# A gated recurrence beside eight experts on one core: second biases added in the mixing, mixing scales for eight tiles at once, a small decay product on GpSimd

## The chip, the cores and the metric

One core of a Trainium2 chip. Its engines run side by side: TensorE (PE), VectorE (DVE), ScalarE (ACT), GpSimd (POOL) and the queue engine SyncE (SP); each takes its own instructions in order and waits for semaphores. The metric is the device time of one execution in microseconds. All data are float32.

## What is computed

`x` is [8, 512, 256] (4096 rows in 32 tiles of 128). `xn` is `x` normalised over its last dimension. Two branches read it:

```
# recurrence, 16 heads of 16 per sequence, 512 steps
q = silu(xn Wq); k = l2norm(silu(xn Wk)); v = xn Wv
f = sigmoid(xn Wf1 Wf2); a = -k * sigmoid(xn Wgamma) * f
S = S * f[:, None];  S = S + k[:, None] * (a . S + v);  o = q . S
o = o * sigmoid(xn Wog1 Wog2)          # the output gate
s = layernorm(o) * norm_w @ Wo
# experts: softmax, the best 2 of 8, weights cw normalised
out = sum_e cw[:, e] * (gelu(xn W1[e] + b1[e]) @ W2[e] + b2[e])
g = silu(layernorm(out) * gamma + beta)
result = x + s * g
```

## The kernel before, in words

A tile n of the input holds 16 time steps of all 8 sequences. The first stage (to about 225 us) projects tile after tile: TensorE multiplies, ScalarE takes sigmoids, VectorE and GpSimd finish a record of a, f, k, q, v (REC = 80 numbers a head) for each row, and SyncE stores the record (`spill`, L361) and the sigmoid for the output gate (`og_d`, L364) to DRAM. SyncE loads records back as chunks of 16 steps with (sequence, head) on the 128 partitions (`rbh`).

The recurrence runs on VectorE through all of the kernel, in 32 chunks of 8 pairs of steps; g = 0 to 255 counts the pairs. Pairs 0 to 55 are VectorE's alone (`two_steps`, L1166), and the projection's small VectorE work is woven into the first 29. From pair 56 (chunk SHARED = 7) `two_shared_steps` (L1207) runs: VectorE multiplies the state with the first step's factors (L1216) and sums; GpSimd (`decay_and_read`, L304) makes one product of 512 columns, which holds the decayed state and the second step's product, and a product of 512 for the outputs (`read_both`, L324). VectorE sums GpSimd's second half at L1224, after `wait_ge(s_dec, g + 1)`. Several of VectorE's operands lie in PSUM (`home_a`, `home_u`, `home_o`). A chunk's preparation for these pairs is in GpSimd's `prepare_part` (L570) and VectorE's `prepared_rows` (L1143). The sums for the outputs are L1164.

`route` (L1039) picks the experts; GpSimd scatters each row of x twice to its expert's place in DRAM (L502), until about 358 us. Then the experts: 39 tiles of 256 rows, `expert_tile` (L886 on TensorE, L708 on ScalarE). TensorE makes the hidden layer (L891), turns the next tile's rows (L879), makes the second layer for two halves of 128 rows (L903) and adds the second bias by a product whose factors are one row of ones and b2 (L905). ScalarE scales the result by the row's weight into `ysb`, and GpSimd scatters it (`land`, L521) to `y_d`. GpSimd's order is written out when the kernel is built: after the products of pair g it lands a half tile if `(g - 56) * PAIR_STEP + LAND0` has reached LAND0 plus the tile's number times LAND_STEP; these are planned times, with PAIR_STEP 3.7 and LAND_STEP 15.9, and no engine waits for a clock. The rest is landed at pair 223.

Mixing: when all is landed, ScalarE loads `y_d` in groups of 4 tiles (L752). Per pair of tiles j: TensorE adds the two expert rows by identity products (`add_experts`, L914), ScalarE takes sum and square sum (`moments`, L757), GpSimd the scales (`spreads`, L533), ScalarE normalises (`normed`, L771), TensorE turns (`turn_y`), ScalarE takes silu (`silu_g`), TensorE turns back, ScalarE copies to `x_acc` (`turned_back`). All of one j comes before all of the next one, but moments of j + 1 stand between, and after each j the output of two tiles follows. For the outputs, in the last four chunks (from pair 224, counted as s = 0), VectorE in pair 224 + s gates the loaded row of outputs (`gate_o`, L1104), takes its statistics (`out_stats`), and, LAG = 5 tiles behind, multiplies the output projection by the mixed experts (`gated`, L1118, which waits for TensorE's product L959 and the mixing of that tile); ScalarE normalises and copies the turned rows, GpSimd takes the scales (`out_scales`) and adds x (`sum_up`), SyncE loads and stores.

The functions that the change touches, with the line numbers of the profile:

Of the kernel before, what the change touches and what calls it, by code (L numbers as in the profile page):

```python
# [11 lines left out]
P = 128  # L12
# [7 lines left out]
REC = 5 * HD  # L20
A_, F_, K_, Q_, V_ = (HD * n for n in range(5))
# [3 lines left out]
RING = 16  # L25
# [19 lines left out]
YR = 3  # L45
SR = 4
RB = 3
SHARED = 7
LAND0, LAND_STEP = 390.0, 15.9
PAIR_STEP = 3.7  # L50


def build(nc, x, wq, wk, wv, wgamma, wf1, wf2, wog1, wog2, norm_w, wo,
          wg, bg, w1, b1, w2, b2, gamma, beta, out):
    ctx = ExitStack()
    with ctx:
# [6 lines left out]
        def sem(name):  # L63
# [6 lines left out]
        og_d = nc.dram_tensor("og_d", [NT, P, D], F32, kind="Internal").ap()  # L70
# [19 lines left out]
        b2_sb = sb("b2_sb", [1, E, D])  # L90
# [21 lines left out]
        ogs = work[:, o1 + 6 * D:o1 + 10 * D].rearrange("p (u n) -> p u n", u=RS)  # L112
        ksq = work[:, o1 + 10 * D:o1 + 11 * D]
# [37 lines left out]
        prod_a = sb("prod_a", [P, NP, 3, HD, ROW])  # L151
# [12 lines left out]
        home_a = psT[1][:, 0:NP * HD].rearrange("p (n k) -> p n k", n=NP)  # L164
# [3 lines left out]
        oTs = xTs  # L168
        sel = gw[:, 0, :, :].rearrange("p t e -> p (t e)")
        b2_flat = b2_sb[:, :, :].rearrange("a e n -> a (e n)")  # L170
        f_on = work[:, 0:FR * D].rearrange("p (u d) -> p u d", u=FR)
        fog, fx, f_sg = (work[:, (FR + n * SL) * D:(FR + (n + 1) * SL) * D].rearrange("p (u d) -> p u d", u=SL)
                         for n in range(3))
# [23 lines left out]
        s_og = sem("s_og")  # L197
# [11 lines left out]
        s_ogd = [sem(f"s_ogd{n}") for n in range(RS)]  # L209
# [10 lines left out]
        s_b1t = sem("s_b1t")  # L220
        s_b1 = sem("s_b1")
# [30 lines left out]
        s_o = sem("s_o")  # L252
        s_od = [sem(f"s_od{n}") for n in range(OB)]
        s_fl = [sem(f"s_fl{n}") for n in range(SL)]
        s_mul = sem("s_mul")
# [25 lines left out]
        N_W, N_C = 10, 9  # L281
# [18 lines left out]

        def over_v(row):
            return row.unsqueeze(1).broadcast_to([P, HD, HD])


        def decay_and_read(eng, g):
            n, u = g % NP, g // NP % RB
            wide = [P, 2, HD, HD]
            rows = rbh[:, u, 2 * n:2 * n + 2, :].rearrange("p j c -> p (j c)")[:, F_:2 * REC - F_ + 2 * A_]
            rows = rows.rearrange("p (j c) -> p j c", j=2)[:, :, 0:HD]
            eng.tensor_tensor(prod_a[:, n, 1:3, :, 0:HD], state[:, g % SR, :, :].unsqueeze(1).broadcast_to(wide),  # L310
                              rows.unsqueeze(2).broadcast_to(wide), ALU.mult).then_inc(s_dec, 1)
# [20 lines left out]
        def _(sp):  # L332
# [40 lines left out]
            def store_chunk(c):  # L373
                sp.dma_start(o_w[c], obh[:, c % OB, :, :]).then_inc(s_od[c % OB], 16)
# [945 lines left out]
```

## Time and profile before

| | us |
|---|---|
| median of 3 runs | 1239.25 (1235.51 to 1239.74) |
| the profiled execution | 1238.9, its span 1237.2 |
| VectorE busy | 1119.4 (90%), 3502 instructions |
| TensorE busy | 938.7 (76%) |
| GpSimd busy | 918.9 (74%), products of 512 columns at 1.27 each (L310 x200, L327 x175) |
| ScalarE busy | 395.7 (32%) |
| second bias, L905 | 156 instructions |

The span is 40 slices of 31 us in the page; a digit is the busy share in tenths:

```profile
PE   5798898100029999999999999999999934667663
DVE  3799999999999999999999999999999995988882
POOL 3766666367844888888888888888888884877762
PEclk9888988655559999999999999999999976777787
```

TensorE works in slices 12 to 31 (the experts), VectorE from slice 1 on; in the last eight slices, the mixing and the outputs, no engine is full, and TensorE's granted clock is 0.6 to 0.8 of 2.4 GHz.

### The profile page before, as it was taken

The page shows a single profiled execution, that of the slowest core. Times are in us where ns is not written, and L with a number is a line of the kernel's source. Part 1 is how long each engine was busy: PE and PEld are TensorE (multiplying, and loading weights), DVE is VectorE, ACT ScalarE, POOL GpSimd, SP SyncE. Part 2 cuts the span into 40 slices and gives each one's busy share as a digit, 9 for nine tenths or more (in the row PEclk, how much of TensorE's full clock was granted, in tenths as well). Part 3 has the DMA queues.
Part 4 walks back from the last instruction along what each step waited for, and adds up shares of the span by engine and source line. Part 5 has one row for each costly group of instructions (what it writes and reads, how often), then busy time and mean ns, then how long its engine had stood idle before and what let it go on. Part 6 is the DMA issues. An engine that isn't in the chain of part 4 may idle for free.

```text
span 1237.2 us, 17465 instructions
## 1 busy us (share of the span) xinstructions
PE 938.7 (76%) x3773; PEld 683.6 (55%) x3774; DVE 1119.4 (90%) x3502; ACT 395.7 (32%) x1047; POOL 918.9 (74%) x902
## 2 busy tenths in 40 slices
PE   5798898100029999999999999999999934667663
PEld 2343343000018888778888777888878723445441
DVE  3799999999999999999999999999999995988882
ACT  3444444200003333332232223333322203554552
POOL 3766666367844888888888888888888884877762
PEclk9888988655559999999999999999999976777787
DMA  5666656553335666655666556666666427355322
GB/s 165 194 209 177 213 180 188 140 191 107 111 94 150 191 196 195 195 170 183 191 195 193 174 177 195 196 187 181 183 192 191 120 67 210 93 157 149 99 81 69
DMA packets 247251, 202.60 MB, mean 164 GB/s; under 512 B 141425, under 2 KB 225233, under 8 KB 247185
## 3 DMA queue, kind: packets, MB, share of 16 engines
q1 hardware_dynamic: 170146, 82.81, 25.5%
q10 hardware_dynamic: 70224, 100.49, 24.8%
q0 software_dynamic: 6816, 18.69, 4.6%
q14 instruction: 55, 0.45, 0.1%
q8 instruction: 10, 0.16, 0.1%
HBM read 139.42 MB, written 62.54 MB: 163 GB/s over the span
## 4 chain that ended last, share of the span: by engine, by line
POOL 36%; DVE 27%; issue 16%; PE 7%; DMA 6%; SPq 3%; ACT 3%; POOLq 0%; DVEq 0%; ACTq 0%
POOL prod_q L327 13%; POOL prod_a L310 12%; POOL y_d L530 5%; DMA rec_d<-work 4%; DVE obh L1164 3%; PE psA L959 3%; DVE ubuf L1180 3%; DVE prod_a L1175 2%; PE psF L921 2%; SPq L335 2%; DVE prod_q L316 1%; DVE prod_a L1198 1%; DVE state L1204 1%; DVE outer L1190 1%; POOL cross L583 1%
## 5 line engine op out<-in xcount | busy, mean ns | idle before, releaser
L310 POOL TENSOR_TENSOR prod_a<-state,rbh 128x512 f32<-128x512 f32 x200 | 254.7, 1274 | 96.2 <-DVE state L1237 74.0
L903 PE MATMUL psF<-wts,work 128*128 128x256 f32 x1248 | 289.1, 385 | 3.2 <-ACT work L712 2.0
L891 PE MATMUL psA<-xgT,wts 128*128 128x256 f32 x1248 | 282.3, 384 | 0.9 <-ACT xgT L706 0.8
L891 PEld LDWEIGHTS psA<-xgT,wts 128*128 128x128 f32 x1248 | 235.4, 191 | 45.1 <-issue 13.8
L903 PEld LDWEIGHTS psF<-wts,work 128*128 128x128 f32 x1248 | 230.8, 190 | 50.0 <-issue 16.5
L327 POOL TENSOR_TENSOR prod_q<-state,rbh 128x512 f32<-128x512 f32 x175 | 223.2, 1276 | 0.0
L1164 DVE TENSOR_REDUCE obh<-prod_q 128x16 f32<-128x272 f32 x512 | 217.6, 426 | 0.0
L712 ACT ACTIVATE work<-psA,b_sb 128x256 f32<-128x256 f32 x312 | 130.8, 470 | 162.3 <-PE psA L891 159.5
L1224 DVE TENSOR_REDUCE ubuf<-prod_a 128x16 f32<-128x272 f32 x200 | 86.0, 430 | 37.5 <-POOL prod_a L310 37.1
L723 ACT ACTIVATE work<-psF,work 128x256 f32<-128x256 f32 x78 | 36.9, 473 | 256.9 <-PE psF L905 256.9
L879 PE MATMUL psT<-ident,work 128*128 128x128 f32 x156 | 24.2, 279 | 119.2 <-DMA work<-xs_d 119.1
L484 POOL TENSOR_TENSOR rinv<-ssm,neghalf 128x16 f32<-128x16 f32 x32 | 100.3, 3134 | 2.7
L502 POOL DMA_INDIRECT xs_d<-x_acc,idx x64 | 79.2, 1237 | 19.5 <-issue 18.9
L1237 DVE TENSOR_TENSOR state<-psB,outer 128x256 f32<-128x256 f32 x200 | 84.2, 421 | 5.8
L1216 DVE TENSOR_TENSOR prod_a<-state,psT 128x256 f32<-128x256 f32 x200 | 83.8, 419 | 5.8
L879 PEld LDWEIGHTS psT<-ident,work 128*128 128x128 f32 x156 | 19.2, 143 | 125.6 <-issue 117.9
L530 POOL DMA_INDIRECT y_d<-work,ids x78 | 78.9, 1011 | 12.3 <-issue 10.0
L1219 DVE TENSOR_REDUCE psB<-prod_a 128x16 f32<-128x272 f32 x200 | 86.5, 432 | 0.0
L1222 DVE TENSOR_TENSOR psB<-rbh,psB 128x256 f32<-128x256 f32 x200 | 83.6, 418 | 0.0
L1230 DVE TENSOR_TENSOR psB<-prod_a,psB 128x256 f32<-128x256 f32 x200 | 83.4, 417 | 0.0
L1232 DVE TENSOR_TENSOR outer<-rbh,psB 128x256 f32<-128x256 f32 x200 | 82.4, 412 | 0.0
L845 PE MATMUL psA<-w_kq,xTs 128*128 128x512 f32 x128 | 78.4, 743 | 0.0
(171 smaller groups left out, 1543.3 us busy)
## 6 DMA issues: line engine op xcount, KB each, us to landing
wts<-in_L_ffn_W_dram ACTq DMA_DIRECT2D x78, 1024.0 KB
rec_d<-work SPq DMA_DIRECT2D x32, 640.0 KB
rbh<-rec_d SPq DMA_DIRECT2D x32, 640.0 KB
xs_d<-zero SPq DMA_DIRECT2D x26, 387.0 KB, 9.0
work<-xs_d ACTq DMA_DIRECT2D x39, 258.0 KB
wts<-y_d ACTq DMA_DIRECT2D x16, 512.0 KB, 5.5
x_acc<-in_L_attn_x_dram SPq DMA_DIRECT2D x32, 128.0 KB
og_d<-work SPq DMA_DIRECT2D x32, 128.0 KB, 7.9
```

The source lines that it names most:

```text
L310: eng.tensor_tensor(prod_a[:, n, 1:3, :, 0:HD], state[:, g % SR, :, :].unsqueeze(1).broadcast_to(wide), rows.unsqueeze(2).broadcast_to(wid ...
L327: eng.tensor_tensor(prod_q[:, g % SR, :, :, 0:HD], state[:, g % SR, :, :].unsqueeze(1).broadcast_to(wide), rbh[:, u, 2 * n - 1:2 * n + 1, ...
L484: pool.tensor_tensor(rinv[:, u, :], ssm[:, u, :], neghalf[:, 0:H], ALU.pow).then_inc(s_ng, 1)
L530: pool.indirect_dma_start(y_d, bass.IndirectOffsetOnAxis(ids[:, v, q:q + 1], 0), ysb[v][:, q, :], None).then_inc(s_yd[v], 16)
L712: act.activation(hT[:, m, :], psA[m // 2 % 2][:, m % 2 * MT:(m % 2 + 1) * MT], ACT.Gelu, bias=b1_sb[:, bass.ds(e * FC + m, 1)]).then_inc(s ...
L891: mm = pe.matmul(psA[m // 2 % 2][:, m % 2 * MT:(m % 2 + 1) * MT], w1_sb[v][:, c, m * P:(m + 1) * P], xgT[:, c, :], start=(c == 0), stop=(c ...
L903: pe.matmul(psF[q][:, 0:D], hT[:, m, q * P:(q + 1) * P], w2_sb[v][:, m, :], start=(m == 0), stop=False)
L1164: dve.tensor_reduce(obh[:, c % OB, row % RING, :], prod_q[:, g % SR, side, :, :], AX.X, ALU.add).then_inc(s_o, 1)
L1216: dve.tensor_tensor(prod_a[:, n, 0, :, 0:HD], old, over_v(home_a[:, n, :]), ALU.mult).then_inc(s_chain, 1)
L1219: dve.tensor_reduce(u1, prod_a[:, n, 0, :, :], AX.X, ALU.add).then_inc(s_chain, 1)
L1224: dve.tensor_reduce(raw, prod_a[:, n, 2, :, :], AX.X, ALU.add).then_inc(s_chain, 1)
L1237: dve.tensor_tensor(new, home_o, outer[:, 1, :, :], ALU.add).then_inc(s_chain, 1)
```

## The change

Its parts:

1. b2 is no longer added in `expert_tile`. It lies 4 times per tile group in `b2_sb` [128, 4, 256], zero elsewhere, loaded by 16 small DMAs that SyncE issues after those of the weights and ahead of the first `spill`. `route` also makes the full weights cw of each row; ScalarE and TensorE turn them into `cwT`, and `add_experts` starts each tile's sum with a product of all 128 rows of `cwT` and `b2_sb`.
2. Mixing goes by groups of GQ = 8 tiles. `moments` copies the sum to `x_acc`, so that PSUM is free after the squares; `spreads(q)` makes the scales of eight tiles in one go, at planned times (SPREADS); `normed` reads `x_acc`. The order on ScalarE is: moments of 16 tiles; then for each q: normalise 8 tiles, moments of the 8 tiles two groups on, silu and turning back. The outputs of the first 8 tiles stand beside the silu of the last group (q = 3), the others behind it.
3. In shared pairs VectorE makes both steps' products itself (512 columns), GpSimd only the decayed state (`decay`, 256 columns, into `decayed`). `two_steps` and `two_shared_steps` become one function.
4. The output gate travels in the record (REC = 96), with one sigmoid of 512 columns in place of two of 256. It is applied to a chunk's outputs at once (`gate_outputs`, 256 columns), by VectorE in the chunks up to 7 and the last one, by GpSimd in the others, at the fourth pair of the next chunk; storing a chunk and loading another into its place wait for that. `og_d`, its stores and loads and `gate_o` are gone.
5. PAIR_STEP becomes 3.86, LAND_STEP 15.0; `out_scales` comes one pair later on GpSimd.

```diff
-REC = 5 * HD
-A_, F_, K_, Q_, V_ = (HD * n for n in range(5))
+REC = 6 * HD
+A_, F_, O_, K_, Q_, V_ = (HD * n for n in range(6))
+GQ = 8
+SPREADS = (612.0, 624.0, 640.0, 662.0)
-LAND0, LAND_STEP = 390.0, 15.9
-PAIR_STEP = 3.7
+LAND0, LAND_STEP = 390.0, 15.0
+PAIR_STEP = 3.86
...
+        def gate_outputs(eng, c):
+            eng.tensor_tensor(obh[:, c % OB, :, :], obh[:, c % OB, :, :], rbh[:, c % RB, :, O_:O_ + HD], ALU.mult)\
+                .then_inc(s_og, 1)
-        def decay_and_read(eng, g):
+        def decay(eng, g):
             n, u = g % NP, g // NP % RB
+            eng.tensor_tensor(decayed[:, :, :], state[:, g % SR, :, :], over_v(rbh[:, u, 2 * n, F_:F_ + HD]),
+                              ALU.mult).then_inc(s_dec, 1)
...
-            sp.dma_start(b2_sb[:, :, :], b2.rearrange("(a e) n -> a e n", a=1)).then_inc(s_c, 16)
+            sp.wait_ge(s_pool0, 5)
+            for n in range(P // E):
+                sp.dma_start(b2_sb[n * E:(n + 1) * E, n % 4, :], b2).then_inc(s_c, 16)
...
             def spill(n):
                 u4 = n % RS
-                sp.wait_ge(s_og, n + 1)
-                sp.dma_start(og_d[n], ogs[:, u4, :]).then_inc(s_ogd[u4], 16)
...
-            def spreads(j):
-                lo, hi = 2 * j, 2 * j + 2
+            def spreads(q):
+                lo, hi = q * GQ, (q + 1) * GQ
...
+                if g % NP == GATED and g // NP > SHARED:
+                    pool.wait_ge(s_o, g // NP * RING)
+                    gate_outputs(pool, g // NP - 1)
                 s = g - WOVEN * NP
+                if spread < NT // GQ and ((g - SHARED * NP) * PAIR_STEP >= SPREADS[spread] or s >= 2):
+                    spreads(spread)
+                    spread += 1
...
+            for j in range(2 * half):
+                moments(j)
+            for q in range(NT // GQ):
+                act.wait_ge(s_yr, q + 1)
+                for j in range(q * half, (q + 1) * half):
+                    normed(j)
+                for j in range((q + 2) * half, min((q + 3) * half, NT // 2)):
+                    moments(j)
+                for j in range(q * half, (q + 1) * half):
+                    silu_g(j)
+                    if q < NT // GQ - 1:
+                        if j > q * half:
+                            turned_back(j - 1)
+                    else:
+                        n = 2 * (j % half)
                         out_normed(n)
+                        out_normed(n + 1)
                         out_turned(n)
+                        turned_back(j)
+                        out_turned(n + 1)
...
-                    pe.matmul(psF[q][:, 0:D], ones[0:1, :], b2_flat[:, bass.ds(e * D, D)], start=False, stop=True)\
-                        .then_inc(s_y, 1)
...
                 for n in range(2 * j, 2 * j + 2):
+                    total = sums[j % 2][:, n % 2 * D:(n % 2 + 1) * D]
+                    pe.matmul(total, cwT[:, n // 4, :], b2_sb[:, n % 4, :], start=True, stop=False)
                     for c in range(2):
+                        mm = pe.matmul(total, ident[:, :], yab[:, g % YR, c, n % GM, :], start=False, stop=(c == 1))
...
+                dve.tensor_tensor(prod_a[:, n, :, :, 0:HD], old.unsqueeze(1).broadcast_to([P, 2, HD, HD]),
+                                  coef.unsqueeze(2).broadcast_to([P, 2, HD, HD]), ALU.mult).then_inc(s_chain, 1)
...
+                if homed:
+                    for j, side in enumerate((u1, raw)):
+                        dve.tensor_reduce(side, prod_a[:, n, j, :, :], AX.X, ALU.add).then_inc(s_chain, 1)
...
                 dve.wait_ge(s_dec, g + 1)
+                dve.tensor_tensor(out1, decayed[:, :, :], out1, ALU.add).then_inc(s_chain, 1)
```

## Rows read from the trace of the kernel before

**Rows 1.** Busy us by stretch: PE, PEld, DVE, ACT, POOL, then PE's granted clock, DMA share, GB/s.

```profile
1010.00:1040.00 30.00, 8.96 (x28) 7.12 (x29) 22.66 (x73) 8.57 (x26) 19.60 (x23) 0.61 0.58 158
1100.00:1150.00 50.00, 34.98 (x117) 25.80 (x117) 43.95 (x147) 25.43 (x74) 40.80 (x53) 0.71 0.50 147
```

**Rows 2.** VectorE's timeline, shared pairs: start us, us, engine, line, operation.

```profile
385.06 0.42 DVE L1216 TENSOR_TENSOR prod_a<-state,psT 128x256 f32<-128x256 f32 x1
...
505.61 0.42 DVE L1216 TENSOR_TENSOR prod_a<-state,psT 128x256 f32<-128x256 f32 x1
...
508.72 0.42 DVE L1237 TENSOR_TENSOR state<-psB,outer 128x256 f32<-128x256 f32 x1
509.17 0.42 DVE L1216 TENSOR_TENSOR prod_a<-state,psT 128x256 f32<-128x256 f32 x1
...
1009.10 0.42 DVE L1216 TENSOR_TENSOR prod_a<-state,psT 128x256 f32<-128x256 f32 x1
```

**Rows 3.** TensorE's timeline in one expert tile, around the second bias.

```profile
507.44 0.69 PE L905 MATMUL psF<-b_sb,ones 1*128 x2
508.06 3.72 PE L903 MATMUL psF<-wts,work 128*128 128x256 f32 x16
```

**Rows 4.** Groups by line: busy us, mean ns, idle us before them and its releasers.

```profile
L1224 DVE TENSOR_REDUCE ubuf<-prod_a 128x16 f32<-128x272 f32 x200 | 86.0, 430 | 37.5 <-POOL prod_a L310 37.1
...
L1216 DVE TENSOR_TENSOR prod_a<-state,psT 128x256 f32<-128x256 f32 x200 | 83.8, 419 | 5.8
...
L1175 DVE TENSOR_TENSOR prod_a<-state,rbh 128x512 f32<-128x512 f32 x56 | 37.9, 677 | 0.1
...
L1106 DVE TENSOR_TENSOR work<-work 128x256 f32<-128x256 f32 x32 | 19.7, 617 | 17.2 <-DMA work<-og_d 17.1
...
L321 POOL TENSOR_TENSOR prod_q<-state,rbh 128x256 f32<-128x256 f32 x25 | 18.1, 724 | 0.0
...
L470 POOL TENSOR_TENSOR rstd<-var,neghalf 128x8 f32<-128x8 f32 x3 | 4.9, 1642 | 0.0
```

**Rows 5.** SyncE's and VectorE's timelines before the first pair.

```profile
28.62 0.45 SPq L354 DMA_DIRECT2D b_sb<-in_L_ffn_b_dram  x1
...
31.45 0.63 SPq L368 DMA_DIRECT2D rec_d<-work  x1
37.97 0.36 SPq L371 DMA_DIRECT2D rbh<-rec_d  x1
...
48.22 0.23 DVE L1130 TENSOR_TENSOR cross<-rbh 128x128 f32<-128x128 f32 x1
```

**Rows 6.** The last landing on GpSimd and the first sums on TensorE.

```profile
1012.60 1.01 POOL L530 DMA_INDIRECT y_d<-work,ids  x1 [0.17 <-issue]
...
1024.71 5.79 PE L921 MATMUL psF<-wts,ident 128*128 128x256 f32 x16 [23.94 <-DMA wts<-y_d]
```

**Rows 7.** ScalarE's and TensorE's timelines, two tiles of mixing and two of output.

```profile
1110.30 1.02 ACT L784 ACTIVATE gT<-psT,gb 128x256 f32<-128x256 f32 x2
...
1113.39 2.07 PE L959 MATMUL psA<-wo_sb,xTs 128*128 128x256 f32 x4 [0.47 <-ACT xTs L801]
...
1116.68 1.03 ACT L776 ACTIVATE wts<-psF,ysh,yrs 128x256 f32<-128x256 f32 x2
1119.88 0.38 ACT L763 ACTIVATE junk<-psF 128x256 f32<-128x256 f32 x1 [2.18 <-PE psF L921]
...
1121.91 1.02 ACT L784 ACTIVATE gT<-psT,gb 128x256 f32<-128x256 f32 x2
```

**Rows 8.** VectorE's timeline in the woven pairs 230, 239 and 240, and its last.

```profile
1062.59 0.41 DVE L1216 TENSOR_TENSOR prod_a<-state,psT 128x256 f32<-128x256 f32 x1
...
1108.17 0.41 DVE L1216 TENSOR_TENSOR prod_a<-state,psT 128x256 f32<-128x256 f32 x1
1112.47 0.41 DVE L1216 TENSOR_TENSOR prod_a<-state,psT 128x256 f32<-128x256 f32 x1
...
1209.74 0.41 DVE L1123 TENSOR_TENSOR work<-psA,x_acc 128x256 f32<-128x256 f32 x1
```

More of the change, by code:

```diff
@@ L398, in _ @@
                 sp.wait_ge(s_yd[u], 16 * MH * ((NM + 1 - u) // 2))
-            for u in range(RS):
-                sp.wait_ge(s_ogd[u], 16 * (NT // RS))
             def fetch(n):
@@ L684, in _ @@
             act.wait_ge(s_b1, 1)
+            act.wait_ge(s_cw, 1)
+            act.activation(cw4.rearrange("p n (r k) -> p n r k", r=4),
+                           gw[:, 1, :, :].rearrange("p (n t) e -> p n (t e)", t=4).unsqueeze(2).broadcast_to([P, NT // 4, 4, 4 * E]),
+                           ACT.Copy).then_inc(s_cw4, 1)
+            act.wait_ge(s_cwT, 1)
+            for n in range(2):
+                act.activation(cwT[:, 4 * n:4 * n + 4, :].rearrange("p n t -> p (n t)"), psA[n][:, :], ACT.Copy, scale=0.25)\
+                    .then_inc(s_cws, 1)
             act.wait_ge(s_slot, 2)
@@ L688, in _ @@
                 act.wait_ge(s_recd[u], 16 * (NT // RS))
-            for u in range(RS):
-                act.wait_ge(s_ogd[u], 16 * (NT // RS))
             def expert_of(t):
@@ L872, in _ @@
             pe.matmul(psT[1][:, 0:NT * E], ones[:, :], sel, start=True, stop=True).then_inc(s_cnt, 1)
+            pe.wait_ge(s_cw4, 1)
+            for n in range(NT // 4):
+                mm = pe.transpose(psA[n // 4][:, n % 4 * P:(n % 4 + 1) * P], cw4[:, n, :], ident[:, :])
+            mm.then_inc(s_cwT, 1)
             pe.wait_ge(s_slot, 2)
+            pe.wait_ge(s_cws, 2)
             def turn_rows(t, v, nth):
@@ L960, in out_rows @@
                 mm.then_inc(s_s, 1)
[L962 to L971 removed]
+            half = GQ // 2
+            for j in range(2 * half):
+                add_experts(j)
+            for q in range(NT // GQ):
+                for j in range((q + 2) * half, min((q + 3) * half, NT // 2)):
+                    add_experts(j)
+                for j in range(q * half, (q + 1) * half):
+                    turn_y(j)
+                    turn_back(j)
+                    if q == NT // GQ - 1:
+                        for n in range(2 * (j % half), 2 * (j % half) + 2):
+                            out_rows(n)
+            for n in range(GQ, NT):
                 out_rows(n)
@@ L1184, in two_steps @@
                     sum_row(g - 2, 0)
-                dve.wait_ge(s_chain, done + 2)
-                dve.scalar_tensor_tensor(out=u2, in0=u1, scalar=pair[:, 1, n:n + 1], in1=u2, op0=ALU.mult, op1=ALU.add)\
+                if shared(g):
+                    sum_row(g - 2, 1)
+                dve.wait_ge(s_chain, done + 3)
+                dve.scalar_tensor_tensor(out=u2, in0=u1, scalar=pair[:, 1, n:n + 1], in1=raw, op0=ALU.mult, op1=ALU.add)\
                     .then_inc(s_chain, 1)
-                dve.tensor_tensor(outer[:, 0, :, :], over_v(rbh[:, u, 2 * n, K_:K_ + HD]), over_k(u1), ALU.mult).then_inc(s_chain, 1)
@@ L1234, in two_shared_steps @@
                 if out_tile is not None and out_tile < NT - 1:
                     out_stats(out_tile)
-                dve.wait_ge(s_chain, done + 8)
-                dve.tensor_tensor(new, home_o, outer[:, 1, :, :], ALU.add).then_inc(s_chain, 1)
+                dve.wait_ge(s_chain, done + 7)
+                dve.tensor_tensor(new, out1, outer[:, 1, :, :], ALU.add).then_inc(s_chain, 1)
+                if not shared(g) and g > 1:
+                    sum_row(g - 2, 1)
                 if out_tile is not None and out_tile >= LAG:
```

233 lines of the change are left out of this document (93 added, 140 removed).

## The prediction

> **What bounds the kernel now.** I read the engine shares of the page first: VectorE is busy 90% of the span, TensorE 76%, GpSimd 74%. Then the stages. In the page's 40 slices TensorE and VectorE both stand at nine tenths while the experts run (365 to 1001 us), with VectorE and GpSimd sharing the recurrence. After that neither is full: at 1010 to 1040 us VectorE works 22.7 of 30 us, TensorE 9, and TensorE's granted clock is 0.61; at 1100 to 1150 it is 0.71 [rows 1]. There a pair of time steps takes VectorE 5 to 7 us instead of 3.56. So I followed three clocks: how fast VectorE goes through its 256 pairs of steps, when the last expert rows land, and how long the mixing takes (sum of two expert rows, LayerNorm, silu, turned back), since `gated` makes VectorE wait for the mixing inside the recurrence.
>
> I number pairs g = 0 to 255. Pair 56 (first one shared with GpSimd) starts at 385.06, pair 221 at 1009.10: 3.782 us a pair [rows 2]. A pair without a wait takes 3.56 (505.61 to 509.17), the chunk's preparation adds 1.0 per 8, and the rest, 0.1, is VectorE waiting for GpSimd's product, 37.1 us over the run [rows 2, 4].
>
> **The second bias.** Two fp32 instructions per half tile go, 0.62 us from the first to what follows (507.44 to 508.06), so 1.24 us in each of 39 tiles, 48 us of TensorE [rows 3]. A tile goes by some 16.2 us now; at 15.0 TensorE's last one ends 47 us earlier than 1001, plus what its start is later, by 960. But what lands is paced by GpSimd, which is told 15.0 us a tile from 390: the last two rows go at pairs 204 and 205. In exchange each mixed tile gets one more product with 128 rows, half of what the two identity products are: 2 instructions of 0.22 (the experts' pitch [rows 3]) to 0.45, hidden until the mixing starts.
>
> **VectorE per shared pair.** The first product becomes 512 wide: 677 ns in the stretch where VectorE works alone, against 419 for the one of 256: +0.26 [rows 4]. The other instructions keep their number and sizes. Before, an instruction stood right behind the one it needs twice, at 0.45 from start to start (508.72 to 509.17) instead of 0.33 [rows 2]; now the small product stands between the sum and the new state, so one of these gaps goes. 3.56 + 0.26 - 0.12 = 3.70 to 3.72; with a preparation of 1.0 per chunk (its copy from 128 to 256 columns is 0.1 more, the rest of the chunk's edge as before) 3.845 a pair. GpSimd's decay product shrinks from 512 to 256 columns (0.72 [rows 4]), a gating of the same size is added once a chunk, and VectorE needs the product only 2.8 us into the pair, where it was 1.7: I cost its waits at 0, and at the 0.1 of now if I am wrong. So a pair goes from 3.782 to 3.845: the lighter GpSimd pays for nearly all of the dearer VectorE.
>
> The SBUF page is to be weighed here. The new product reads the state in SBUF and its factors in PSUM beside GpSimd, as the one of 256 did, which took 419 ns in the mean of 200, hardly above the 0.41 of its best [rows 4, 8]: no slowing, so +0.26 stands. (Held by one GpSimd product each time, it would be 0.7 a pair, 140 us; the nearest row says no.) Only the removed gating of a loaded row (`gate_o`, both inputs in SBUF) shows it: 617 ns in the mean [rows 4]. The Trainium skill ("SBUF — State Buffer", section "SBUF: two separate sides") says a VectorE operation with two SBUF inputs and a GpSimd operation exclude each other for a whole instruction; the trace agrees. By that rule the change takes one such case out of each woven pair and adds none.
>
> **Before pair 56.** The sync queue must issue 16 loads for the second bias where one was, each some 0.45 us [rows 5], ahead of the first record's store. That store went at 31.45, its load at 37.97, and VectorE used it at 48.22 without a wait [rows 5]. I put the store at 37.8 and the load, after a record larger by a fifth, at 45. What the load takes isn't shown: with 3 us VectorE isn't late, with 10 it is late by 7. I take 4. Then 6 gatings of a chunk by 0.35 before pair 56 (2.1) and one at pair 59, and the added products of `route`, of which 0.4 are left since VectorE waits there for TensorE anyhow. The two sigmoids in one and the output gates without their own store save ACT and the sync queue work, which VectorE hides: 0, and 2 us at most where records are late around 60 us. Pair 56 starts at 385.06 + 4 + 2.1 + 0.4 = 391.6.
>
> **The mixing.** Landing at pair 205: 391.9 + 149 x 3.845 = 965, and 2 us of products. Before, 12.1 us lay between the last landing's issue (1012.60) and TensorE's first sum (1024.71) [rows 6]; now the first sum is at 979. Pairs of tiles then pass their moments while TensorE does 12 instructions (2.8 us, the first 5.4): all of the first eight are through by 1008, which hides them beside VectorE. But the scales of the first eight tiles are taken by GpSimd at pair 215: 391.9 + 159 x 3.845 = 1003.3, plus its products (1.95) and 2.4 for the scales (the power over 8 columns is 1.64 [rows 4], two small ones around it): 1007.7. From there ScalarE and TensorE alternate in one chain, in an order in which **the first output tile comes after three quarters of the mixing**: `gated(0)`, which VectorE does in pair 229, needs
>
> - normalising 16 pairs of tiles at 0.93 (1.03 for two with their tail overlapped [rows 7]): 14.9
> - moments of the last 8 pairs at 2.1 (1119.88 to 1121.91): 17, and TensorE's cold start in each group of four, 3 each: 23 [rows 6, 7]
> - one load of ScalarE's function table, which I take with 1.3
> - 12 turns of silu: silu 0.93, the previous pair's copy back 0.55, TensorE turns back and turns the next one (1.1 to 1.9 by the clock), handing over 0.3: 2.9 to 3.6, I take 3.2: 38.4; the durations are those of the chain in [rows 7]
> - silu of pair 12, and the first output row: 1110.30 to 1115.46 in the trace: 5.2 [rows 7]
>
> together 82.8, so `gated(0)` at 1090.5. VectorE by its own pace is at pair 224 at 1038 and would want it at 1064: it stands for some 26 us. In the kernel before, pair 230 starts at 1062.59 [rows 8]; now at 1090.9, 28 later.
>
> **The woven pairs after it.** A pair with neither wait nor statistics takes 4.30 now (1108.17 to 1112.47) [rows 8]. The wide product adds 0.26, `gate_o` takes 0.33 away: 4.24; statistics' scales 0.71 per 4 pairs and preparation 1.0 per 8: 4.55. ScalarE and TensorE need 8.4 us for two tiles without moments and normalising (1110.30 to 1121.91 less 3.2 for those), against 9.1 of VectorE, so VectorE sets the pace, where before the chain of 11.6 us per two tiles did. 26 x 4.55 = 118.3: the last pair ends at 1209.2, against 1210.07 before (from pair 230, 147.5) [rows 8]. So the gain of 29 in this stretch pays back the stand of 28. Behind it: gating the last chunk and its wait +0.8, the gate load and `gate_o` of the last tile -0.45. Span 1237.2 - 0.9 + 0.35 = 1236.7. The profiled execution was 1238.9 for its span of 1237.2, 0.35 below the median 1239.25, and I leave that out: **1238 us, no change** that can be measured (about 0.5%, 6 us, is what can be told).
>
> **Rivals.**
> - *The chain of mixing is shorter.* With TensorE at 2.4 GHz in it the turns are 2.7 (-6), the moments 18 (-5), and if the first load isn't late, -4: 1223 to 1228. For it: the 16 first sums take 5.79 [rows 6], so 0.36 each, already between the two clocks after a gap of 24 us. Against: the granted clock was 0.61 and 0.71 in this stage [rows 1], with gaps as now. Chance 0.27.
> - *VectorE never stands at `gated(0)`.* Then pair 230 starts at 1064, and 118.3, 27.5 for what follows the last pair (1237.2 - 1210.07 + 0.35) and 1.7 outside the span give 1212. It needs the 83 us chain done in 56; ScalarE's own work in it is some 60. Chance 0.05.
> - *Slower: the chain is longer*, TensorE at 1.2 GHz through it: turns 3.6 (+5), sums of 5.4 us a pair in the moments (+7), scales of the third or fourth eight tiles late (GpSimd, in order, holds VectorE at pair 226), and the recurrence's start late by 7 (+3). It decides from a chain of 89 us: 1246, and all of it 1253. For it: TensorE runs only short bursts between ScalarE's steps. Chance 0.28.
> - *The 48 us of TensorE reach the end.* That would be 1191. It can't be while the landing waits for pairs of the recurrence; under 0.01.
>
> **Numbers.** Forecast case 0.40, its own range 1233 to 1245. Range of all 1225 to 1252: below lie the case without a stand and a fifth of the first rival, above some of the slower one. Faster than 1233: 0.32; within 0.5%: 0.40; above 1245: 0.28.
>
> **What would show it.** An expert tile of 14.7 to 15.0 us; first product of 0.60 and 3.85 us a pair between pairs 60 and 200, with almost no wait of VectorE for GpSimd; pair 56 at 389 to 395; TensorE idle for some 20 us before 979; ScalarE waiting for the scales until 1008; one wait of VectorE of 20 to 32 us in `gated` at pair 229, for TensorE's output product; 4.5 to 4.7 us a pair behind it. I am wrong if that wait is under 12 us, or if woven pairs stay above 5 us.

## The result, and the profile after

The changed kernel takes 1257.79 us in the median (1256.94 to 1259.01) against 1239.49 for the kernel before beside it: 1.0153 times, 95% interval 1.0136 to 1.0170. I had forecast 1238, and 1225 to 1252 as the range: it is slower by 18 us and lies 6 us above that range. Its profiled execution took 1259.01 with a span of 1257.3, 20.1 longer than before.

Three words are used below. The *stand* is the one long idle time of VectorE at `gated(0)`, in pair 229. *Woven* pairs are those from 224 on, which carry the work on the outputs. A *chunk's edge* is the last pair of a chunk with the preparation of the next.

The page of the changed kernel, busy shares and VectorE's line by slices:

```profile
PE 902.5 (72%) x3689; PEld 684.2 (54%) x3689; DVE 1163.9 (93%) x3482; ACT 403.0 (32%) x1018; POOL 819.5 (65%) x891
...
DVE  3779999999999999999999999999999998299993
```

TensorE has 36 us less to do, GpSimd 99 less, VectorE 44.5 more. In the slices at 1037 to 1069 and 1069 to 1100 us VectorE falls to 8 and 2 tenths: the second is the stand. Behind it VectorE is full again, where it was at 8 and 9 before.

Groups of the changed kernel by line (busy us, mean ns | idle before), to set beside [rows 4]:

```profile
L1206 DVE TENSOR_TENSOR prod_a<-state,psT 128x512 f32<-128x512 f32 x200 | 137.3, 687 | 6.0
...
L1237 DVE TENSOR_TENSOR psB<-decayed,psB 128x256 f32<-128x256 f32 x200 | 84.8, 424 | 2.9 <-POOL decayed L315 2.9
L1175 DVE COPY prod_a<-rbh 128x256 f32<-128x256 f32 x24 | 19.6, 815 | 0.0
L1008 DVE TENSOR_TENSOR lt<-stats 128x4 f32<-128x4 f32 (+3 forms) x14 | 8.6, 617 | 0.0
```

The first product costs 687 against 419, as planned, and VectorE's wait for GpSimd went from 37.1 us to 2.9. The last two groups were no terms of my sum.

VectorE's timeline: pairs 56, 57, 215, 216, 229, what it stood for there, and pairs 230 and 231 (compare [rows 2, 8]):

```profile
396.95 0.69 DVE L1206 TENSOR_TENSOR prod_a<-state,psT 128x512 f32<-128x512 f32 x1
400.65 0.69 DVE L1206 TENSOR_TENSOR prod_a<-state,psT 128x512 f32<-128x512 f32 x1
...
1012.31 0.69 DVE L1206 TENSOR_TENSOR prod_a<-state,psT 128x512 f32<-128x512 f32 x1
...
1074.06 0.69 DVE L1206 TENSOR_TENSOR prod_a<-state,psT 128x512 f32<-128x512 f32 x1
...
1102.00 0.42 DVE L1148 TENSOR_TENSOR work<-psA,x_acc 128x256 f32<-128x256 f32 x1 [23.95 <-PE psA L981]
1102.34 0.68 DVE L1206 TENSOR_TENSOR prod_a<-state,psT 128x512 f32<-128x512 f32 x1
1106.58 0.68 DVE L1206 TENSOR_TENSOR prod_a<-state,psT 128x512 f32<-128x512 f32 x1
```

So pair 56 is at 396.95 (I said 391.6), a plain shared pair is 3.70 as predicted, 159 pairs take 3.870 each (3.845), the stand at `gated(0)` is there and 24 us long (20 to 32), but it ends at 1102.0 and not at 1090.5. A plain woven pair is 4.24, as predicted (1102.34 to 1106.58). Yet the stretch from 1102.34 to the end of the last pair, at 1231.27, is 128.9 and not 118.3.

One thing here belongs to this one execution. Eighteen of the 19 chunk's edges between pairs 56 and 215 take 4.99 to 5.00 us and one, at 674 us, takes 6.67, because a copy in it lasts 2.49 and not 0.82:

```profile
674.41 2.49 DVE L1175 COPY prod_a<-rbh 128x256 f32<-128x256 f32 x1
```

Of the experiments below, those that leave these pairs as they are take 3.857 or 3.858 us a pair and not 3.870. So 1.9 us of every "earlier than the changed kernel" that is read behind pair 215 come from the profile that it is compared with.

The hand-over to the mixing, on GpSimd and ScalarE:

```profile
1016.42 0.22 POOL L543 TENSOR_TENSOR ysh<-ynm,yrs 128x8 f32<-128x8 f32 x1
```

```profile
1009.65 0.20 ACT L780 ACTIVATION_READ_ACCUMULATOR junk<-psF,ynm 128x1 f32 x1
1016.68 3.55 ACT L787 ACTIVATE wts<-x_acc,ysh,yrs 128x256 f32<-128x256 f32 x7 [6.84 <-POOL ysh L543]
```

ScalarE had done the moments of sixteen tiles and then stood 6.84 us for scales that GpSimd makes behind pair 215. From there the chain takes 85.3 us to 1102.0; I had 82.8 from 1007.7.

Set against my sum of 1236.7: scales 9.0 late (5.4 from the start, 3.6 from the pairs, about half of it that one edge), chain +2.5, woven stretch +10.6, tail -1.5 (26.0 us after 1231.27, I had 27.5) make 1257.3. The experiments take these terms, and the stand itself, one by one.

### The profile page after: what moved, and what is told of

The parts are those of the page before. It is cut to its first block, busy times and chain, and to the rows that moved or that the text cites. A ratio compares the mean times of both kernels' runs of the same rounds, so it can differ in the third digit from the quotient of the medians.

```text
span 1257.3 us, 17142 instructions
## 1 busy us (share of the span) xinstructions
PE 902.5 (72%) x3689; PEld 684.2 (54%) x3689; DVE 1163.9 (93%) x3482; ACT 403.0 (32%) x1018; POOL 819.5 (65%) x891
## 4 chain that ended last, share of the span: by engine, by line
DVE 66%; issue 18%; DMA 4%; PE 4%; POOL 3%; ACT 3%; SPq 1%; DVEq 0%; POOLq 0%; ACTq 0%
DVE obh L1191 10%; DVE outer L1229 7%; DVE psB L1215 6%; DVE state L1246 6%; DVE psB L1237 5%; DVE ubuf L1215 5%; DVE prod_a L1206 4%; DMA rec_d<-work 3%; DVE prod_q L1240 3%; DVE ubuf L1217 3%; DVE psB L1225 2%; DVE prod_a L1175 1%; DVE prod_q L321 1%; DVE outer L1237 1%; DVE work L1038 1%
## 5 line engine op out<-in xcount | busy, mean ns | idle before, releaser
L315 POOL TENSOR_TENSOR decayed<-state,rbh 128x256 f32<-128x256 f32 x200 | 145.4, 727 | 227.9 <-DVE state L1246 204.4
L927 PE MATMUL psF<-wts,work 128*128 128x256 f32 x1248 | 277.5, 381 | 0.0
L916 PEld LDWEIGHTS psA<-xgT,wts 128*128 128x128 f32 x1248 | 237.7, 192 | 37.1 <-ACT work L722 4.5
L927 PEld LDWEIGHTS psF<-wts,work 128*128 128x128 f32 x1248 | 235.8, 191 | 30.3
L1206 DVE TENSOR_TENSOR prod_a<-state,psT 128x512 f32<-128x512 f32 x200 | 137.3, 687 | 6.0
L1237 DVE TENSOR_TENSOR psB<-decayed,psB 128x256 f32<-128x256 f32 x200 | 84.8, 424 | 2.9 <-POOL decayed L315 2.9
L1215 DVE TENSOR_REDUCE ubuf<-prod_a 128x16 f32<-128x272 f32 x200 | 85.3, 427 | 0.0
L865 PE MATMUL psA<-w_kq,xTs 128*128 128x512 f32 x128 | 82.4, 778 | 0.0
```

The source lines that it names most:

```text
L315: eng.tensor_tensor(decayed[:, :, :], state[:, g % SR, :, :], over_v(rbh[:, u, 2 * n, F_:F_ + HD]), ALU.mult).then_inc(s_dec, 1)
L916: mm = pe.matmul(psA[m // 2 % 2][:, m % 2 * MT:(m % 2 + 1) * MT], w1_sb[v][:, c, m * P:(m + 1) * P], xgT[:, c, :], start=(c == 0), stop=(c ...
L927: mm = pe.matmul(psF[q][:, 0:D], hT[:, m, q * P:(q + 1) * P], w2_sb[v][:, m, :], start=(m == 0), stop=(m == FC - 1))
L1206: dve.tensor_tensor(prod_a[:, n, :, :, 0:HD], old.unsqueeze(1).broadcast_to([P, 2, HD, HD]), coef.unsqueeze(2).broadcast_to([P, 2, HD, HD] ...
L1215: dve.tensor_reduce(side, prod_a[:, n, j, :, :], AX.X, ALU.add).then_inc(s_chain, 1)
L1237: dve.tensor_tensor(out1, decayed[:, :, :], out1, ALU.add).then_inc(s_chain, 1)
```

## The experiments

Each is the changed kernel with one edit, if nothing else is said. The ratios are to the kernel before, which stood beside them at 1239.86 us (biases, statistics, gating, copies), 1240.51 (`out_scales`), 1242.28 (the doubled decay product, one run of each) and 1240.96 (the others). A gain in us is the difference from the changed kernel's 1257.79, which had 1239.49 beside it. The kernel before thus moved by up to 1.5 us between the series of several runs, and reckoned against it each gain comes out larger, by 0.4 to 1.5 us.

### The loads of the second bias behind the last record

```diff
-            for n in range(P // E):
-                sp.dma_start(b2_sb[n * E:(n + 1) * E, n % 4, :], b2).then_inc(s_c, 16)
...
+            for n in range(P // E):
+                sp.dma_start(b2_sb[n * E:(n + 1) * E, n % 4, :], b2).then_inc(s_b2, 16)
```

The loop leaves its place ahead of the first record's store and stands behind the last record.

> The changed kernel with the 16 loads of the second bias issued by SyncE after the last record instead of ahead of the first. Theory: these loads make the first records late, and the 10 us that the changed kernel is behind at pair 4 (84.55 against 74.59 us) go nearly whole; since the wait of VectorE in pair 229 hangs on the scales taken at pair 215, the end comes earlier by the same: 1248 to 1250 us against 1258. Rival: the larger records (768 KB against 640) make the stores land later, so that half of the 10 us or more stays: 1252 to 1256.

SyncE of the changed kernel, what [rows 5] showed of before, and VectorE's waits:

```profile
28.89 5.91 SPq L361 DMA_DIRECT2D b_sb<-in_L_ffn_b_dram  x16
...
36.75 0.63 SPq L372 DMA_DIRECT2D rec_d<-work  x1
44.28 0.38 SPq L375 DMA_DIRECT2D rbh<-rec_d  x1
```

```profile
DVE work L1038 <- DMA rec_d<-work: 9.7, 3, 6.5
```

The same two views of this experiment:

```profile
31.13 0.63 SPq L371 DMA_DIRECT2D rec_d<-work  x1
38.64 0.38 SPq L374 DMA_DIRECT2D rbh<-rec_d  x1
```

```profile
DVE work L1041 <- DMA rec_d<-work: 4.4, 2, 4.2
```

1250.42 us (1249.15 to 1251.68), ratio 1.0083 [1.0061, 1.0105]: 7.4 less than the changed kernel. Pair 56 comes at 390.91, 6.0 earlier, and every stage behind it moves with it. Of the 10.0 us at pair 4 (84.55 against 74.59), 5.7 go (78.89) and 4.3 stay, so the loads were a little more than half of it and not nearly the whole, as I had expected; the rival's larger records are the likely rest. So sixteen small DMAs on a queue that feeds VectorE cost their full 6 us. My sum had let VectorE absorb some of that, because the first load had not been waited for. But the wait falls on later records: VectorE waits for a record's store to leave the slot in `work` (L1038), in all 9.7 us. With the loads gone 4.4 us of it stay; before it was 0.5. What has changed there besides is the record, a fifth larger, so I put these down to it; no run took it back by itself.

### The output scales told before the new state

```diff
+                for q, (lo, hi) in enumerate(NORMS):
+                    if out_tile is not None and out_tile == hi - 1 and hi < NT:
+                        out_spread(q)
                 dve.wait_ge(s_chain, done + 7)
                 dve.tensor_tensor(new, out1, outer[:, 1, :, :], ALU.add).then_inc(s_chain, 1)
...
-                for q, (lo, hi) in enumerate(NORMS):
-                    if out_tile is not None and out_tile == hi - 1 and hi < NT:
-                        out_spread(q)
```

> The changed kernel with VectorE's out_spread (seven small instructions, in every fourth woven pair) issued ahead of the new state instead of behind it, where GpSimd stands idle. Theory: the two additions of two SBUF inputs (0.59 and 0.69 to 1.23 us now, 0.15 before the change) are held by GpSimd's products, which start when the state is ready; ahead of it they take 0.15 to 0.17, and 7 or 8 times 1.1 to 1.5 us go: 1247 to 1250 us. Rival: what VectorE waits for is not GpSimd's use of SBUF, or the state comes later by as much: 1256 to 1259.

VectorE of the changed kernel in `out_spread`, and GpSimd beside it:

```profile
1130.89 0.59 DVE L1006 TENSOR_TENSOR lt<-stats 128x4 f32<-128x4 f32 x1
1131.40 0.15 DVE L1007 TENSOR_TENSOR lt<-stats 128x4 f32<-128x4 f32 x1
1131.47 1.23 DVE L1008 TENSOR_TENSOR lt<-stats 128x4 f32<-128x4 f32 x1
...
1132.70 0.70 DVE L1013 TENSOR_SCALAR nmean<-lt 128x4 f32<-128x4 f32 x1
```

```profile
1130.73 0.72 POOL L315 TENSOR_TENSOR decayed<-state,rbh 128x256 f32<-128x256 f32 x1 [0.92 <-DVE state L1246]
1131.42 1.27 POOL L332 TENSOR_TENSOR prod_q<-state,rbh 128x512 f32<-128x512 f32 x1
1132.65 0.73 POOL L584 TENSOR_TENSOR cross<-rbh 128x256 f32<-128x256 f32 x1
```

VectorE of the experiment in the same place:

```profile
1125.75 0.17 DVE L1006 TENSOR_TENSOR lt<-stats 128x4 f32<-128x4 f32 x1
...
1125.91 0.16 DVE L1008 TENSOR_TENSOR lt<-stats 128x4 f32<-128x4 f32 x1
...
1126.06 0.17 DVE L1013 TENSOR_SCALAR nmean<-lt 128x4 f32<-128x4 f32 x1
```

1246.38 us (1244.12 to 1249.94), ratio 1.0055 [1.0036, 1.0074]: 11.4 less. Seven statistics instructions of four elements fell from 2.69 us to 0.70 (1125.75 to the new state at 1126.45) without one of them being changed. Read the two engines against each other: L1006 ends (1131.48) when GpSimd's decay product does (1131.45), L1008 (1132.70) with GpSimd's product of 512 columns (1132.69), L1013 (1133.40) with the one after (1133.38). Before the new state GpSimd has nothing to multiply, and they pass. In the eight groups of the changed kernel in pairs 227 to 254 L1006 takes 0.58 to 0.69 and L1008 0.69 or 1.23 each time, and L1013 0.69 to 1.23 in six of them. From pair 230 to 255 the experiment takes 114.8 us, the changed kernel 125.0.

### GpSimd's output scales one pair earlier again

In the kernel before, the small instructions stood in the same place of VectorE's program, and took 0.14 to 0.17 in all their groups. What differed is GpSimd. VectorE and GpSimd of the kernel before in the pair that ends at 1096.95:

```profile
1095.93 0.15 DVE L981 TENSOR_TENSOR lt<-stats 128x4 f32<-128x4 f32 x1
```

```profile
1096.79 1.11 POOL L561 TENSOR_TENSOR rstd<-var,neghalf 128x4 f32<-128x4 f32 x1 [5.45 <-DVE var L1116]
```

GpSimd had been idle for 5.45 us, waiting for these very statistics ahead of the next pair's products. The change moved that wait behind them. Undone alone, on GpSimd only:

```diff
-                        if s == hi:
+                        if s == hi - 1 and s < NT - 1:
                             out_scales(q)
```

> The changed kernel with GpSimd's scales of the outputs (`out_scales`) one pair of steps earlier again, as in the kernel before; VectorE's program is not touched. Theory (the wait of GpSimd for the statistics was what kept its products away from VectorE's small adds): the small adds fall from 0.58 to 1.23 us back to 0.15 to 0.17, the pairs with output statistics go from 6.4 to 7.4 us to 4.9 to 6.1, GpSimd's decay product starts 1.3 us later in the next pair and is still in time; time 1247 to 1249. Rival (the place in VectorE's program alone counts, behind the new state): no change, 1256 to 1259. Second rival (the decay product after the scales comes too late and VectorE waits for it): small adds short, time 1252 to 1256.

```profile
1128.52 0.15 DVE L1006 TENSOR_TENSOR lt<-stats 128x4 f32<-128x4 f32 x1
```

```profile
1129.37 1.02 POOL L563 TENSOR_TENSOR rstd<-var,neghalf 128x4 f32<-128x4 f32 x1 [2.62 <-DVE var L1141]
```

1247.83 us (1246.21 to 1249.43), ratio 1.0056 [1.0038, 1.0073]: 10.0 less, without an instruction of VectorE moved. From pair 230 to 255 it takes 114.4. The decay product behind the scales is nearly in time: VectorE's waits for it come to 2.6 us. So this and the experiment before it remove the same cost by two ways; no run has both. My prediction's front had the edit ("`out_scales` comes one pair later on GpSimd"), and my sum had it at nothing.

### The gating taken later and caught up

```diff
+GATES = [max(0, min(s - LAG + 1, (3 * (s - 10)) // 2)) for s in range(32)]
...
-                if out_tile is not None and out_tile >= LAG:
-                    gated(out_tile - LAG)
+                for n_out in due(out_tile) if out_tile is not None else ():
+                    gated(n_out)
```

(`due(s)` is range(GATES[s - 1], GATES[s]); stores, loads of x and `sum_up` follow it.)

> The changed kernel with the gating of the outputs begun at pair 235 (s = 11) instead of 229, then 3 tiles in 2 pairs until it is 5 behind again at pair 247; adding x and storing follow it. Theory: VectorE stands 24 us at pair 229 only because the first output tile is asked for before the mixing chain has reached it (1102 us). Asked for later, the stand shrinks to under 5 us and the end comes 15 to 24 us earlier: 1234 to 1243 us. Rival: the chain of mixing and output on ScalarE and TensorE sets the end, and the time that VectorE gains it loses again at its gatings: 1252 us or more.

VectorE's wait for TensorE's output product from 1050 us on (in all, times, longest), the changed kernel and then the experiment:

```profile
DVE work L1148 <- PE psA L981: 36.0, 4, 23.9
```

```profile
DVE work L1159 <- PE psA L992: 14.6, 4, 8.9
```

1235.34 us (1233.46 to 1237.16), ratio 0.9965 [0.9949, 0.9980]: 22.5 less, the largest of all, with the same work in another order. Pair 230 starts at 1075.26, not 1102.34 (27.1 earlier). Some of it is lost again: the gatings that are caught up crowd the pairs behind it (pair 255 at 1202.44, 24.9 earlier; the span 24.3 shorter). The longest stand left is 8.9 us, where I had expected under 5.

### The two copies of the chunk's edge in their old order

```diff
-                dve.tensor_copy(home_a, rbh[:, u, :, A_:A_ + HD]).then_inc(s_prep, 1)
                 dve.tensor_copy(prod_a[:, :, :, :, HD]..., rbh[:, u, :, V_:V_ + HD]).then_inc(s_prep, 1)
+                dve.tensor_copy(home_a, rbh[:, u, :, A_:A_ + HD]).then_inc(s_prep, 1)
```

> The changed kernel with the two copies at a chunk's start in the order of the kernel before (the values' column into prod_a first, the factors into PSUM second). Theory: the copy from SBUF to SBUF takes 0.82 us instead of 0.39 because GpSimd's product has begun by then; first, it is over before: a chunk's edge falls from 4.99 to about 4.65 us, pair 215 comes 6 to 7 us earlier and the end 5 to 8: 1250 to 1253 us. Rival: the order changes nothing, as the other copy or the sum waits instead: 1256 to 1259.

VectorE of the changed kernel, then of the experiment, at the same chunk:

```profile
612.23 0.42 DVE L1174 COPY psT<-rbh 128x256 f32<-128x256 f32 x1
612.55 0.82 DVE L1175 COPY prod_a<-rbh 128x256 f32<-128x256 f32 x1
```

```profile
610.23 0.38 DVE L1174 COPY prod_a<-rbh 128x256 f32<-128x256 f32 x1
610.44 0.49 DVE L1176 COPY psT<-rbh 128x256 f32<-128x256 f32 x1
```

1249.98 us (1249.25 to 1251.64), ratio 1.0080 [1.0060, 1.0100]: 7.8 less. A chunk's edge takes 4.64 us and not 4.99, which is 6.7 over the 19 up to pair 215. In the profiles pair 215 is 8.4 earlier, at 1003.92 (3.816 a pair for 3.870); the other 1.7 are the one copy of 2.49. The copy from SBUF into SBUF takes 0.38 where it starts ahead of GpSimd's decay product (610.23 against 610.39), and 0.82 in second place, when that product has begun (612.40). The copy into PSUM takes 0.42 and 0.49 in the two places: it can go second. My 1.0 for the edge had the lengths of the kernel before, but the changed kernel has not its order.

### The first scales of mixing three pairs earlier

```diff
-SPREADS = (612.0, 624.0, 640.0, 662.0)
+SPREADS = (600.0, 624.0, 640.0, 662.0)
```

> The changed kernel with one number changed: the scales of the first eight mixed tiles taken three pairs of steps earlier (pair 212, not 215). Theory (the scales' place in GpSimd's order holds the chain of mixing: ScalarE waited 6.84 us until 1016.68 for moments that were done at 1009.9): GpSimd waits at pair 212 until 1009.9 and has the scales at 1012.3, 4.4 us earlier; VectorE waits 5 to 7 us for GpSimd's decay product at pair 213, which it gives back out of its stand at pair 229; time 1253.5 (1251 to 1255). Rival (the chain is held by the later scales or by VectorE, so that the wait only moves): 1257 to 1260.

GpSimd's last scale and what ScalarE does with it:

```profile
1004.10 0.21 POOL L543 TENSOR_TENSOR ysh<-ynm,yrs 128x8 f32<-128x8 f32 x1
```

```profile
1008.78 4.03 ACT L787 ACTIVATE wts<-x_acc,ysh,yrs 128x256 f32<-128x256 f32 x8
```

1250.21 us (1248.85 to 1252.20), ratio 1.0075 [1.0057, 1.0093]: 7.6 less, more than the 4.3 expected. The direction was right, the reason half wrong: the scales of eight tiles need four pairs' moments, which were done by 999, not the sixteen tiles' of 1009.9, so GpSimd waited for nothing. All of ScalarE's 6.84 us went, and its moments ended 1.1 earlier besides, since the landings move with the recurrence, which is 1.9 earlier at pair 215 (the one long edge of the profile that it is compared with).

### The four edits together, and with earlier scales

Biases, `out_spread`, gating and copies as in their experiments, in one kernel:

> Four edits to the changed kernel at once: the 16 loads of the second bias behind the last record, output scales told before the pair's new state, the gatings of the output shifted by up to ten pairs and caught up, the two copies of the chunk's edge in their old order. Theory (each removes a cost of its own: 6 us of start, 0.04 us a pair from 56 to 215, the stand of 28 us at pair 229 and the wait of the woven pairs for GpSimd's port): pair 56 at 391, pair 215 at 998 (0.054 a pair less than 3.870 and 6 earlier), no stand over 9 us, pair 230 at 1061, 117 for the 25 woven pairs and 30 behind them: span 1208, time 1210 (1205 to 1222). Rival (the chain of ScalarE and TensorE becomes the end as soon as VectorE's costs go, so the gains don't add up): 1222 to 1233, no better than the late gatings alone by more than 12.

1212.17 us (1211.53 to 1214.90), ratio 0.9775 [0.9758, 0.9793]. Singly the four gave 7.4, 11.4, 22.5 and 7.8, together 49.1; in one kernel 45.6. So they are in the main four costs and not four views of one. Pair 56 is at 392.24, 215 at 998.81, 230 at 1061.02, 255 at 1179.36.

With the first scales at pair 213 as well:

> The four edits of the run before in this list together with the earlier scales (the first eight at pair 213, not 215). Theory: with the late gatings there is no stand for the chain of mixing to shorten, so this gives nothing beside the four edits: the same time within 3 us. Rival (ScalarE's and TensorE's chain still sets the woven pairs): 4 us faster than those.

1208.03 us (1206.04 to 1209.51), ratio 0.9732 [0.9715, 0.9750]. I had expected nothing, and the rival's 4 us came. Part of that is the start of this run, with pair 56 at 391.04, 1.2 earlier; but pair 227 waits for GpSimd and the port no more (4.85 against 6.89), and by pair 255 it is 3.1 ahead. This is the fastest kernel here, 33 us faster than the one before the change and 50 faster than the changed one.

### What the 48 us of TensorE are worth

The kernel before, without the second bias of the experts (left out altogether) and with LAND_STEP = 15.0:

```diff
-                    pe.matmul(psF[q][:, 0:D], ones[0:1, :], b2_flat[:, bass.ds(e * D, D)], start=False, stop=True)\
-                        .then_inc(s_y, 1)
+                    mm.then_inc(s_y, 1)
...
-LAND0, LAND_STEP = 390.0, 15.9
+LAND0, LAND_STEP = 390.0, 15.0
```

> The kernel before with the second bias of the experts left out altogether (two fp32 instructions less in each half tile; the output lacks that bias) and the expert rows told to land every 15.0 us, not 15.9. It tells what 48 us less of TensorE are worth by themselves. Theory (the landing goes earlier, but the scales of mixing and all of the output stay behind pair 224 of the recurrence, and VectorE's pairs are unchanged): last landing near 972, first sums near 985, pair 221 at 1009 as before, time 1234 to 1240. Rival (TensorE's time reaches the end): 1192 to 1215.

TensorE's first sums, to compare with [rows 6]:

```profile
982.92 6.57 PE L919 MATMUL psF<-wts,ident 128*128 128x256 f32 x16 [32.88 <-DMA wts<-y_d]
1021.18 1.12 PE L931 MATMUL psT<-ident,wts 128*128 128x128 f32 x4 [31.69 <-ACT wts L776]
```

1229.73 us (1228.86 to 1231.79), ratio 0.9913 [0.9896, 0.9929]: 11 us faster than the kernel before, 4 below the range I gave, and far from the rival's 1192 to 1215. The last expert tile starts 49 us earlier (942.75 for 992.04) and the first sum 42; then TensorE idles 31.7 us for the first scales, which hang on the recurrence's pair 224. What reaches the end comes by way of the recurrence: pair 215 is 3.9 earlier, pair 224 7.4, pair 230 10.3. The run has the bias and the landing step changed together, so it prices both and not the bias alone.

### GpSimd's decay product done twice

```diff
+            if shared(g):
+                eng.tensor_tensor(spare[:, :, :], state[:, g % SR, :, :], over_v(rbh[:, u, 2 * n, F_:F_ + HD]), ALU.mult)
```

> The changed kernel with GpSimd's decay product of every shared pair done twice, first into a buffer that nobody reads: 0.7 us more of GpSimd in each pair. Theory (VectorE's work of a pair runs beside GpSimd unhindered, and GpSimd had 1.06 us of idle time a pair): a plain shared pair stays at 3.70 to 3.72; the copy of 256 columns from SBUF to SBUF at the chunk's edge, held until GpSimd's product ends, goes from 0.82 to 1.5; pairs with landings or preparation of GpSimd wait up to 0.6. In the mean 3.95 to 4.00 a pair, 13 to 20 us by pair 215, and the small instructions of the output statistics are held no longer than now or one product more each (up to +10); time 1270 to 1290. Rival (busy GpSimd slows VectorE's wide products too): a plain pair of 4.0 or more and over 1300. Second rival (slack covers it all): within 3 us of 1257.8.

The group of its copies, and a chunk's edge on VectorE and on GpSimd:

```profile
L1179 DVE COPY prod_a<-rbh 128x256 f32<-128x256 f32 x24 | 24.4, 1016 | 0.0
```

```profile
866.32 2.97 DVE L1179 COPY prod_a<-rbh 128x256 f32<-128x256 f32 x1
```

```profile
866.27 0.72 POOL L317 TENSOR_TENSOR spare<-state,rbh 128x256 f32<-128x256 f32 x1
...
868.33 0.71 POOL L330 TENSOR_TENSOR prod_q<-state,rbh 128x256 f32<-128x256 f32 x1
```

One run, 1277.06 us, and its pair rate is what counts: 3.958 in the mean over pairs 56 to 215 (expected 3.95 to 4.00), plain pairs still 3.70, VectorE's wide products unchanged. So GpSimd's slack covers most of 0.7 us more a pair, and VectorE's products that read one SBUF and one PSUM operand are not held. What the 14 us up to pair 215 consist of: 7.3 are waits of VectorE for the decay product, where GpSimd has a landing or a preparation to do, and about as much are longer edges (5.48 in the mean for 5.08). The copy isn't held for one product more each time, as I wrote: in the 24 chunks ten times 0.81, nine times 0.38, once 0.92 and four times 2.97, through all four products that GpSimd has without a gap (866.27 to 869.04).

## Why the prediction was wrong, step by step

- **The pair's arithmetic: right.** 0.687 for the wide product (0.68), 3.70 a plain pair (3.70 to 3.72), 2.9 us of waits for GpSimd (0), 4.24 woven (4.24).
- **"The chunk's edge as before": wrong.** The edge takes 4.99 us where my 3.845 a pair allows some 4.8, and over 159 pairs that is 1.7 us (3.6 in the profiled execution). The copy alone is 0.4 longer than it need be. The prediction had the copy's growth and missed its new place behind the other; undone it gave 7.8 us.
- **"Before pair 56 ... I take 4": mis-sized.** The store went at 36.75 (37.8 predicted), the first load was late by only 0.7, and still pair 56 came 11.9 later than before, not 6.5. The delay fell on the slots of later records, and all but 1.9 of it is there at pair 4. Moving the loads gave back 6.0 of it.
- **The landing and the expert tiles: right in kind and too short**, and worth little, as the last rival said. A tile takes 15.28 in the mean (before 16.31; 14.7 to 15.0 predicted) and 14.25 where nothing holds it; one tile of 15.76 (508.34 to 524.10) has a wait of 1.30 for its rows. The last landing's issue is at 976.26 and the first sum at 984.27 (979), behind 14.5 us of idle TensorE (some 20 predicted).
- **The chain of mixing: its length nearly right (85.3 for 82.8), its start 9.0 late.** The scales' 4.4 us behind pair 215 were right; pair 215 was late by the start and the edge. The earlier scales show that this start is the end's: 7.6 us.
- **The stand at `gated(0)`: right in place and cause, and in size by luck.** VectorE came to it at 1078.05 and not at 1064, 14 us late, and the chain ended at 1102.0 and not at 1090.5, 11.5 late: two errors that nearly cancel leave 24 for the 26 predicted. Of the 14 us, 9.0 are the late pair 215 and the rest is pair 227, which takes 10.16: GpSimd is held up in it by the scales of mixing (VectorE waits 2.9 for the decay product), and the output statistics come under its products. The stand was the largest cost and I called it paid back by the woven pairs; nothing in the chain forces it. Taken apart, it is 22.5 us.
- **"118.3 for 26 woven pairs": the failed step.** It is the term that is furthest off (+10.6 of the 20.6 us that the span exceeds my sum; the late start of the chain is 9.0). Plain pairs are 4.24, but those with the output statistics 6.4 to 7.4: 128.9 in all. I had 0.71 for the statistics (and 1.0 for a chunk's edge), the length they had while GpSimd stood still, and I put the move of `out_scales` at nothing. With that move undone, or with the statistics ahead of the new state, pairs with statistics take 4.9 to 6.1. The prediction said of the change that by the rule of two SBUF inputs it "takes one such case out of each woven pair and adds none". It adds up to three in each pair with output statistics: `gate_o` is gone (617 ns, [rows 4]), and the small instructions come under GpSimd's products, at up to 1.23 us each. That is 10 to 11 us by either experiment. The Trainium skill ("SBUF — State Buffer", section "SBUF: two separate sides") names both cases in one sentence, VectorE operations with two SBUF inputs (against a GpSimd operation that reads SBUF) and those in a two-port mode, and further down an fp32 copy from SBUF to SBUF as one of the latter; the trace agrees with both, at 1.23 for 0.16 and 0.82 for 0.38. I had applied it to large operations that the change touches, and not to small ones that it leaves alone.

What happened is most like the slower rival (1246 to 1253), though 5 us above even that; its start late by 7 is in it (5.4 behind the forecast, where the rival had 3) and so are its late scales at pair 226 (a wait of 2.9 in pair 227); its main cause, TensorE at 1.2 GHz through the chain, is only a part. In the silu turns it is there: 3.63 a turn for the 3.2 I took, except for the first turn of each four, which is shorter; the twelve take 40.4 us for my 38.4. The granted clock over 1010 to 1040 us is 0.70 of 2.4 GHz (0.61 before, [rows 1]), so TensorE is for a good part at 1.2 GHz there. ScalarE's timeline of two turns, with its waits for TensorE:

```profile
1037.66 1.02 ACT L795 ACTIVATE gT<-psT,gb 128x256 f32<-128x256 f32 x2 [2.06 <-PE psT L955]
...
1041.29 1.02 ACT L795 ACTIVATE gT<-psT,gb 128x256 f32<-128x256 f32 x2 [2.12 <-PE psT L955]
```

What stays open: why the pairs of the kernel before go 0.03 us faster each when its landing does, as the run without the second bias showed (VectorE's wait for GpSimd until 1010 us fell there from 16.1 to 11.4, which is most of the 4.9; what in GpSimd's order does it wasn't tried). Of the 5.9 us before pair 56 that stay when the loads are moved, 4.3 are there at pair 4, before any gating has run, and 1.6 come behind it, where the six gatings of 0.41 to 0.43 us stand; that the 4.3 are the longer record is argued from the waits and not tested.

## What to carry to other kernels

When an engine's order is edited, list not only what its instructions wait for but what runs beside them: a small VectorE operation with two SBUF inputs, or a copy within SBUF, cost 0.15 to 0.4 us here where GpSimd idled, and often lasted as long as GpSimd's product where it didn't, and a wait that looked like waste may have been what kept GpSimd idle. Such operations belong in the gap before the instruction that releases GpSimd. And before an in-order engine waits once for the start of a pipeline, ask whether the waiting instruction could come later: here that was worth 22.5 us, more than the 11 us for 48 us of TensorE's work in the kernel before.

## What the runs showed of the hardware that I had not expected

- The hold is not always one GpSimd instruction long. The same copy took 0.38, 0.82, 2.49 (once in the changed kernel, at 674.41, where three products in a row start 0.15 behind it) and 2.97 us (under four). The rule of one whole instruction, which the prediction went by, is too short for these; what decides between the lengths is open.
- It depends on the moment and on where the operands lie: L1007, of the same size and tiles as L1006 and L1008, passed in 0.15 right behind L1006, where one GpSimd product ends and the next begins. L1010 and L1015 have two SBUF inputs too and took 0.15 to 0.17 in every group, while L1013, with one input, was held with the others: so the form of an operation alone does not tell whether it is held, and in these groups the instruction right behind a held one always passed. Of the copies, the one of 128x256 into PSUM took 0.42 to 0.49 beside the same GpSimd product.
